# A sixteen-head attention with straight code in place of loops, and the out projection of each batch moved into the heads of the next

## The chip, the core and the metric

The kernel runs on one core of a Trainium2 chip. The metric is the device time of one execution in microseconds (us). Engines: TensorE (PE in the profile, PEld its weight loads), VectorE (DVE), ScalarE (ACT), GpSimd (POOL) and SyncE (SP), which issues the DMAs.

## The reference, cut to what matters

The network has four parts: a GRU over 256 time steps, a mixture of experts, an attention and a ternary gated feed-forward. Only the attention, in its wait structure, is changed. Per batch of 8, with 256 tokens, 16 heads of 32:

```python
xn = rms_norm(x, g_norm) * (1.0 + scale) + shift
q, k, v = split(xn @ W_qkv)             # 16 heads, each of width 32
q = rms_norm(q, g_q)
k = rms_norm(k, g_k)
attn = softmax(einsum('bhqd,bhkd->bhqk', q, k) * d ** -0.5)
o = einsum('bhqk,bhkd->bhqd', attn, v)  # -> (b, n, 512)
return o + o @ W_out
```

## The kernel before

The program is written by hand, engine by engine; each engine runs its own list in order, and semaphores couple the lists. The attention is one block of the program (lines 1459 to 1901). Values that need more than 16-bit precision are carried as a high and a low fp16 part, so most steps exist twice: ACT makes the high part (a copy that rounds), DVE or POOL the low part (a subtraction).

The attention goes batch by batch, and `batch(b)` overlaps two of them. For batch b it does the softmax side, head by head: `scores_t(b, h)` (transposed scores, L1547) two heads ahead, exp and its rounding on ACT (`softmax`, L1676 and L1681), the low part on DVE for heads 0 to 7 (`low_p`, L1783) and on POOL for heads 8 to 15 (L1876), then `values(b, h)` (L1562). After each four heads DVE divides by the sums (`normalise`, L1789 and L1791), PE transposes the four heads' outcome (`turn_out`, L1572), ACT and DVE split it (`high_out` L1686, `low_out` L1796). For batch b+1 it does the preparation between the heads, by tables of head numbers: six products of the q, k, v projection at heads 0, 1, 2, 3, 5 and 6 (`project`, L1494, taken out by ACT in `take_out`, L1645), the norms of q and k (with a square root on ACT, L1650, which needs another table than exp), their high and low parts (`high_qk` L1655, `low_qk` L1761 and L1762), the stacking of q and k by transposes at heads 8, 9, 10 and 13 (`stack`: L1512 on PE, q copied by DVE in L1767, k by ACT in L1659), and the row maxima of the scores from head 9 on (`scores` L1528 on PE, `maximum` L1772 on DVE). When all 16 maxima of batch b+1 are there, `turn_max` transposes them (L1534), ACT rounds them (L1664) and a DMA lays them into a row of q (L1467), which `scores_t(b+1, 0)` waits for.

At the end of a batch stands the out projection, in two halves of 24 products (`project_out`, L1586), with `scores_t(b+1, 0)` and `scores_t(b+1, 1)` between them. ACT takes each half out (L1712), DVE makes its low part (L1833). They use banks 5 and 6 of the PSUM, which `project` and `stack` also use:

```python
                    turn_out(b, 3)
                    if not last:
                        turn_max(b + 1)
                    project_out(b, 0, last)
                    if not last:
                        scores_t(b + 1, 0)
                        scores_t(b + 1, 1)
                    project_out(b, 1, last)
```

PE, POOL and SP run 7 batches as a hardware loop and the last as straight code; ACT and DVE loop over 6 and have two as straight code. The tables are `PROJECT_AT`, `STACK_AT`, `MAX_AT` and others, from line 1415.

## Time and profile before

| | us |
|---|---|
| median of 3 runs (lowest, highest) | 1812.58 (1811.27, 1815.29) |
| the profiled execution, its own time | 1806.46 |
| its span | 1804.7 |
| PE busy over the span | 1605.0 (89%) |
| DVE busy | 1182.3 (66%) |
| ACT busy | 918.2 (51%) |
| POOL busy | 599.8 (33%) |
| attention: first product of the projection to the first of the feed-forward | 1110.9 to 1573.4 |
| feed-forward | 1573.4 to 1804.7 |

Times within the span are counted from its start. PEclk is the granted clock of TensorE as a share of full speed: 1.00 is 2.4 GHz, 0.50 is 1.2 GHz. A row of the timeline gives start, duration, engine, line, operation, tile, and in brackets how long the engine had been idle and what ended that.

### The profile page before, as it was taken

Reading aid. Unit: us, or ns where it says so; the run is one execution under the profiler, and the core shown is the slowest. Engines: PE = TensorE matmul, PEld = TensorE weight load, DVE = VectorE, ACT = ScalarE, POOL = GpSimd, SP = SyncE. Lnnn points to the kernel's source line nnn. Section 1 sums busy time; section 2 is a strip of 40 time slices with the busy share of each in tenths; the row PEclk is TensorE's granted clock in tenths of the full one; section 3 lists DMA queues with packets and bytes.
Section 4 is the critical chain, followed back from the end, with each engine's and each line's share of the span. In section 5 each row is a group of like instructions: output and inputs, shape, how many; then the busy total and the mean of one; then the engine's idle time right before and its main releaser. Section 6 shows DMA issues by size and latency. Waiting matters only on the chain. (4 is left out here: it accounts for less than half of the span.)

```text
span 1804.7 us, 77596 instructions
## 1 busy us (share of the span) xinstructions
PE 1605.0 (89%) x32043; PEld 1221.5 (68%) x32043; DVE 1182.3 (66%) x4253; ACT 918.2 (51%) x3325; POOL 599.8 (33%) x1805
## 2 busy tenths in 40 slices
PE   6999999999999999996499956688888888699999
PEld 5999999999999999995366633355555555444444
DVE  5778787887877788886644445566655666573231
ACT  5555555555555566555155444466766666532130
POOL 0333333333333333334355434123322323580000
PEclk9999999999999999555699976788888989699999
DMA  4110101011100111003346352000000000130001
GB/s 171 49 29 8 53 17 45 24 33 42 46 22 5 43 49 46 25 23 117 110 159 237 131 183 98 1 1 0 0 0 0 0 0 1 33 109 18 30 0 47
DMA packets 45708, 90.37 MB, mean 50 GB/s; under 512 B 6736, under 2 KB 25296, under 8 KB 45392
## 3 DMA queue, kind: packets, MB, share of 16 engines
q1 hardware_dynamic: 38992, 64.89, 11.4%
q0 software_dynamic: 6400, 20.98, 3.4%
q8 instruction: 234, 3.83, 0.9%
q14 instruction: 82, 0.67, 0.1%
HBM read 66.90 MB, written 18.87 MB: 48 GB/s over the span
## 5 line engine op out<-in xcount | busy, mean ns | idle before, releaser
L402 PE MATMUL bank<-arena 128*128 128x8 f16 x12288 | 499.6, 170 | 7.6 <-issue 3.3
L405 PE MATMUL bank<-arena 128*128 128x16 f16 x12288 | 495.5, 182 | 2.2 <-issue 1.6
L402 PEld LDWEIGHTS bank<-arena 128*128 128x128 f16 x12288 | 410.1, 97 | 37.0 <-ACT bank L498 22.1
L405 PEld LDWEIGHTS bank<-arena 128*128 128x128 f16 x12288 | 411.6, 97 | 3.7 <-issue 2.6
L664 POOL TENSOR_TENSOR arena<-arena 128x16 f32<-128x16 f32 x512 | 116.7, 228 | 537.9 <-DVE arena L607 523.2
L468 ACT ACTIVATE arena<-arena 128x16 f32<-128x16 f32 x512 | 114.4, 223 | 304.2 <-DVE arena L586 304.0
L597 DVE TENSOR_TENSOR_SCAN arena<-arena,bank 128x64 f32<-128x64 f32 x512 | 147.1, 287 | 19.5 <-ACT arena L468 2.6
L1938 PE MATMUL bank<-arena 128*128 128x512 f16 x704 | 152.3, 379 | 1.7 <-PEq L1459 1.7
L586 DVE TENSOR_REDUCE arena<-bank 128x16 f32<-128x48 f32 x512 | 99.9, 195 | 80.8 <-PE bank L405 76.0
L375 PE MATMUL bank<-arena 128*128 128x256 f16 x1008 | 147.9, 273 | 1.5 <-issue 1.3
L1494 PE MATMUL bank<-arena 128*128 128x512 f16 x576 | 143.8, 405 | 4.5 <-DVE arena L1738 4.5
L603 DVE TENSOR_TENSOR_SCAN arena<-arena 128x48 f16<-128x48 f32 x512 | 134.2, 262 | 6.2 <-ACT arena L478 0.2
L478 ACT ACTIVATE arena<-arena 128x16 f32<-128x16 f32 x512 | 119.2, 233 | 22.9 <-DVE arena L597 4.4
L474 ACT ACTIVATE arena<-arena 128x16 f32<-128x16 f32 x512 | 110.3, 215 | 35.2 <-DVE arena L591 0.9
L1938 PEld LDWEIGHTS bank<-arena 128*128 128x128 f16 x704 | 68.8, 98 | 84.7 <-issue 1.9
L1876 POOL TENSOR_TENSOR arena<-arena 128x512 f16<-128x512 f32 x64 | 79.8, 1256 | 131.1 <-ACT arena L1681 131.0
L591 DVE TENSOR_REDUCE arena<-bank 128x16 f32<-128x48 f32 x512 | 106.2, 207 | 26.1 <-PE bank L405 1.1
L665 POOL COPY arena<-arena 128x16 f32<-128x16 f32 x512 | 118.4, 231 | 0.0
L607 DVE TENSOR_TENSOR_SCAN arena<-arena 128x48 f32<-128x48 f32 x512 | 117.3, 229 | 0.4
L1494 PEld LDWEIGHTS bank<-arena 128*128 128x128 f16 x576 | 59.4, 103 | 73.5 <-issue 16.6
L612 DVE TENSOR_TENSOR arena<-arena 128x16 f16<-128x16 f32 x512 | 95.8, 187 | 17.7
L666 POOL COPY arena<-arena 128x16 f32<-128x16 f32 x512 | 102.7, 201 | 0.0
(203 smaller groups left out, 2708.6 us busy)
## 6 DMA issues: line engine op xcount, KB each, us to landing
arena<-yrows SPq DMA_DIRECT2D x16, 512.0 KB, 4.1
arena<-in_wgu SPq DMA_DIRECT2D x48, 128.0 KB
arena<-in_xT SPq DMA_DIRECT2D x32, 128.0 KB, 2.3
hrows<-arena SPq DMA_DIRECT2D x16, 256.0 KB, 4.0
arena<-in_xtok SPq DMA_DIRECT2D x16, 256.0 KB
out_y<-arena SPq DMA_DIRECT2D x16, 256.0 KB, 2.0
arena<-in_wih SPq DMA_DIRECT2D x4, 768.0 KB, 5.5
arena<-in_whh SPq DMA_DIRECT2D x4, 768.0 KB, 6.0
```

What stands on the lines that cost most here:

```text
L375: mm = nc.tensor.matmul(bank[7][:, half_of(mt)], wihs[:, wp, k, mt, :], xs[:, xp, k, half_of(c)], start=(i % 24 == 0), stop=(i % 12 == 11) ...
L402: mm = nc.tensor.matmul(dst[:, j * B:(j + 1) * B, 1], w, h[:, 0], start=home not in opened, stop=False, skip_group_check=True)
L405: mm = nc.tensor.matmul(dst[:, j * B:(j + 1) * B, 1:3], w, h.rearrange("p a c -> p c a"), start=home not in opened, stop=False, skip_group ...
L468: A.activation(fn[:, HALF[g], 3], rzp[:, 0, HALF[g]], ACT.Sigmoid, scale=1 / SWX).then_inc(r_act[g], 1)
L478: A.activation(inh[:, HALF[g], 0], sn[:, HALF[g], 3], ACT.Tanh, scale=1 / SWX).then_inc(n_act[g], 1)
L597: V.tensor_tensor_scan(flat(sn[:, HALF[g]]), flat(fn[:, HALF[g]]), flat(gate_sums(t, 2, g)), 0.0, ALU.mult, ALU.add).then_inc(n_pre[g], 1)
L603: V.tensor_tensor_scan(flat(mv[:, t % 2, 0, HALF[g]]), flat(fh[:, HALF[g]]), flat(inh[:, HALF[g]]), 0.0, ALU.mult, ALU.add).then_inc(h_hi[ ...
L607: V.tensor_tensor_scan(flat(sh[:, HALF[g]]), flat(fh[:, HALF[g]]), flat(inh[:, HALF[g]]), 0.0, ALU.mult, ALU.add).then_inc(h_f32[g], 1)
L664: G.tensor_tensor(inh[:, HALF[g], 1], zeros[:, :], sh[:, HALF[g], 2], ALU.subtract)
L665: G.tensor_copy(inh[:, HALF[g], 2], sh[:, HALF[g], 2])
L1494: mm = nc.tensor.matmul(bank[5 + i % 2][:, :], xn[:, x_, k, half * P:(half + 1) * P], wqs[:, w_, k, col:col + D], start=(n == 0), stop=(n ...
L1938: mm = nc.tensor.matmul(bank[2 * a + u % 2][:, :], w12[:, mt, a, k, :], o2p[:, 2 * c:2 * c + 2, part, k, :], start=(n == 0), stop=(n == 2 ...
```

## The change

It does five things. (1) The loops of the attention become straight code on all five engines, so waits compare with constants. (2) `project_out(b-1, 0)` now stands at head 4 of batch b, and `project_out(b-1, 1)` at head 7, in banks 4 and 7; the last batch's own two halves stay at its end. (3) ACT and DVE take these halves out at heads 7 and 8 (`high_o2`, `low_o2`). (4) At heads 5, 9 and 13 `turn_out`, `high_out` and `low_out` come after the other work of that head instead of before it. (5) `oTp` has two buffers. The diff without blank lines:

```diff
@@ -1407,3 +1407,3 @@
 m = Mem(arena, mc.at)
-oTp = m.take([2, KT, S], F16)
+oTp = m.take([2, 2, KT, S], F16)
@@ -1419,2 +1419,4 @@
 LOW_AT = {6: (0, 1), 7: (2, 3)}
+OUT_AT = {4: 0, 7: 1}
+O2_AT = {7: (0,), 8: (1,)}
 STACK_AT = {8: (0,), 9: (1,), 10: (2,), 13: (3,)}
@@ -1473,3 +1475,3 @@
         load_max(0)
-        with sp.Fori(0, B - 1) as b:
+        for b in range(B - 1):
             load_max(b + 1)
@@ -1484,3 +1486,3 @@
-                pe.wait_ge(o2_lo, 2 * b + i - 1)
+                pe.wait_ge((qs_done, ks_done)[i], 4 * b)
             elif i >= 2:
@@ -1523,5 +1525,8 @@
                 pe.wait_ge(max_done, H * b + h - 1)
-            elif h == 1 and not first:
+            elif not first:
+                if h == 1:
-                pe.wait_ge(mT_done, b)
+                    pe.wait_ge(mT_done, b)
+                if b > 1:
+                    pe.wait_ge(o2_lo, 2 * (b - 2) + h + 1)
             for qt in range(2):
@@ -1575,3 +1580,3 @@
-        def project_out(b, jp, last):
+        def project_out(b, jp):
             if jp == 0:
@@ -1579,3 +1584,3 @@
-            pe.wait_ge((qs_done, ks_done)[jp], 4 * b + (4 if last else 8))
+                pe.wait_ge(max_done, H * min(b + 2, B))
             for a in range(2):
@@ -1585,4 +1590,4 @@
                     for k in range(KT):
-                        mm = nc.tensor.matmul(bank[5 + jp][:, a * S:(a + 1) * S],
-                                              wos[:, w_, k, j * P:(j + 1) * P], oTp[:, x_, k, :],
+                        mm = nc.tensor.matmul(bank[4 + 3 * jp][:, a * S:(a + 1) * S],
+                                              wos[:, w_, k, j * P:(j + 1) * P], oTp[:, b % 2, x_, k, :],
                                               start=(n == 0), stop=(n == 3 * KT - 1))
@@ -1598,4 +1603,2 @@
                     scores_t(b, h + 2)
-                if h % 4 == 1 and h > 4:
-                    turn_out(b, h // 4 - 1)
                 if not last:
@@ -1607,2 +1610,6 @@
                         scores(b + 1, i)
+                if h in OUT_AT and b > 0:
+                    project_out(b - 1, OUT_AT[h])
+                if h % 4 == 1 and h > 4:
+                    turn_out(b, h // 4 - 1)
                 values(b, h)
@@ -1613,7 +1620,7 @@
                 turn_max(b + 1)
-            project_out(b, 0, last)
-            if not last:
                 scores_t(b + 1, 0)
                 scores_t(b + 1, 1)
-            project_out(b, 1, last)
+            else:
+                project_out(b, 0)
+                project_out(b, 1)
@@ -1630,3 +1637,3 @@
         scores_t(0, 1, True)
-        with pe.Fori(0, B - 1) as b:
+        for b in range(B - 1):
             batch(b, False)
@@ -1685,3 +1692,7 @@
             act.wait_ge(oT_mm, 4 * b + q4 + 1)
-            A.activation(oTp[:, 0, q4, :], bank[q4 % 2][:, 0:S], ACT.Copy).then_inc(oTh_done, 1)
+            A.activation(oTp[:, b % 2, 0, q4, :], bank[q4 % 2][:, 0:S], ACT.Copy).then_inc(oTh_done, 1)
+        def high_o2(b, jp):
+            act.wait_ge(wo_mm, 2 * b + jp + 1)
+            A.activation(o2p_of(b, 0, jp), bank[4 + 3 * jp], ACT.Copy, scale=1 / SW).then_inc(o2_hi, 1)
@@ -1692,4 +1703,2 @@
                     softmax(b, h + 1)
-                if h % 4 == 1 and h > 4:
-                    high_out(b, h // 4 - 1)
                 if not last:
@@ -1703,2 +1712,7 @@
                         stack(b + 1, g)
+                if b > 0:
+                    for jp in O2_AT.get(h, ()):
+                        high_o2(b - 1, jp)
+                if h % 4 == 1 and h > 4:
+                    high_out(b, h // 4 - 1)
             high_out(b, 3)
@@ -1709,5 +1723,5 @@
                 norm_x(b + 2)
-            for jp in range(2):
-                act.wait_ge(wo_mm, 2 * b + jp + 1)
-                A.activation(o2p_of(b, 0, jp), bank[5 + jp], ACT.Copy, scale=1 / SW).then_inc(o2_hi, 1)
+            if last:
+                for jp in range(2):
+                    high_o2(b, jp)
@@ -1726,3 +1740,3 @@
         norm_x(1)
-        with act.Fori(0, B - 2) as b:
+        for b in range(B - 2):
             batch(b, False, True)
@@ -1795,5 +1809,10 @@
             dve.wait_ge(oTh_done, 4 * b + q4 + 1)
-            V.tensor_tensor(oTp[:, 1, q4, :], bank[q4 % 2][:, 0:S], oTp[:, 0, q4, :],
+            V.tensor_tensor(oTp[:, b % 2, 1, q4, :], bank[q4 % 2][:, 0:S], oTp[:, b % 2, 0, q4, :],
                             ALU.subtract).then_inc(oTl_done, 1)
+        def low_o2(b, jp):
+            dve.wait_ge(o2_hi, 2 * b + jp + 1)
+            V.scalar_tensor_tensor(o2p_of(b, 1, jp), bank[4 + 3 * jp], 1 / SW, o2p_of(b, 0, jp), ALU.mult,
+                                   ALU.subtract).then_inc(o2_lo, 1)
         def batch(b, last, more):
@@ -1807,4 +1826,2 @@
                     normalise(b, h // 4 - 1)
-                if h % 4 == 1 and h > 4:
-                    low_out(b, h // 4 - 1)
                 if not last:
@@ -1818,2 +1835,6 @@
                         low_qk(b + 1, n)
+                if b > 0:
+                    for jp in O2_AT.get(h, ()):
+                        low_o2(b - 1, jp)
+                if not last:
                     for g in STACK_AT.get(h, ()):
@@ -1822,2 +1843,4 @@
                         maximum(b + 1, i)
+                if h % 4 == 1 and h > 4:
+                    low_out(b, h // 4 - 1)
             normalise(b, 3)
@@ -1830,8 +1853,5 @@
                 norm_x(b + 2)
-            for jp in range(2):
-                dve.wait_ge(o2_hi, 2 * b + jp + 1)
-                V.scalar_tensor_tensor(o2p_of(b, 1, jp), bank[5 + jp], 1 / SW, o2p_of(b, 0, jp), ALU.mult,
-                                       ALU.subtract).then_inc(o2_lo, 1)
-        V.memset(rk[:, :, :], 0.0).then_inc(o2_lo, 2)
+            if last:
+                for jp in range(2):
+                    low_o2(b, jp)
@@ -1852,3 +1872,3 @@
         norm_x(1)
-        with dve.Fori(0, B - 2) as b:
+        for b in range(B - 2):
             batch(b, False, True)
@@ -1898,3 +1918,3 @@
             squares(0, i)
-        with pool.Fori(0, B - 1) as b:
+        for b in range(B - 1):
             batch(b, False)
```

On PE, heads 4 and 5 of a looped batch (L1494 projection, L1547 transposed scores, L1562 values, L1572 transposes of the outcome; REGISTER_ALU computes what a wait compares with). Before:

```order
L1543 REGISTER_ALU
L1547 MATMUL bank<-arena 128x256 x2
L1556 REGISTER_ALU
L1442 REGISTER_ALU
L1562 MATMUL bank<-arena 128x33 x12
L1543 REGISTER_ALU
L1547 MATMUL bank<-arena 128x256 x2
L1572 MATMUL bank<-cst,arena 128x128 x2
L1488 REGISTER_ALU
L1494 MATMUL bank<-arena 128x512 x12
L1442 REGISTER_ALU
L1562 MATMUL bank<-arena 128x33 x12
```

Now, batch 1, from the values of head 3 on (L1496 projection, L1552 transposed scores, L1567 values, L1577 transposes of the outcome, L1591 out projection):

```order
L1567 MATMUL bank<-arena 128x33 x12
L1552 MATMUL bank<-arena 128x256 x2
L1591 MATMUL bank<-arena 128x256 x24
L1567 MATMUL bank<-arena 128x33 x12
L1552 MATMUL bank<-arena 128x256 x2
L1496 MATMUL bank<-arena 128x512 x12
L1577 MATMUL bank<-cst,arena 128x128 x2
L1567 MATMUL bank<-arena 128x33 x12
L1552 MATMUL bank<-arena 128x256 x2
```

The first half of the out projection stands between `scores_t` and `values` of head 4, and the two transposes of the outcome have gone behind the projection of head 5.

On PE, heads 7 to 9 of batch 1 now (L1514 stacking, L1533 scores for the maxima):

```order
L1552 MATMUL bank<-arena 128x256 x2
L1591 MATMUL bank<-arena 128x256 x24
L1567 MATMUL bank<-arena 128x33 x12
L1552 MATMUL bank<-arena 128x256 x2
L1514 MATMUL bank<-id,arena 96x128 x16
L1567 MATMUL bank<-arena 128x33 x12
L1552 MATMUL bank<-arena 128x256 x2
L1514 MATMUL bank<-id,arena 96x128 x16
L1533 MATMUL bank<-arena 128x256 x4
L1577 MATMUL bank<-cst,arena 128x128 x2
```

The second half of the out projection stands at head 7, ahead of the first stacking; between the two stackings nothing was added on PE.

On DVE, heads 7 and 8 before (L1761 and L1762 low parts of q and k, L1789 and L1791 normalise, L1767 copy of the stacked q, L1796 low part of the outcome):

```order
L1761 COPY arena<-arena 128x16x32
L1762 TENSOR_TENSOR arena<-arena 128x16x32
L1789 RECIPROCAL arena<-bank 128x8
L1790 REGISTER_ALU
L1791 TENSOR_TENSOR arena<-bank,arena 128x2x128
L1767 COPY arena<-bank 96x1024
L1796 TENSOR_TENSOR arena<-bank,arena 128x256
L1767 COPY arena<-bank 96x1024
```

Now (L1775 and L1776, L1803 and L1805, L1781, and L1815 the low part of the out projection):

```order
L1776 TENSOR_TENSOR arena<-arena 128x16x32
L1815 SCALAR_TENSOR_TENSOR arena<-bank,arena 128x512
L1803 RECIPROCAL arena<-bank 128x8
L1805 TENSOR_TENSOR arena<-bank,arena 128x2x128
L1815 SCALAR_TENSOR_TENSOR arena<-bank,arena 128x512
L1781 COPY arena<-bank 96x1024 x2
L1786 TENSOR_REDUCE arena<-bank 128x2 x2
```

The copy of the stacked q stands behind the second L1815, which needs the second high part of ACT. On ACT, heads 8 and 9 now (L1683 and L1688 exp and its rounding, L1697 high part of the out projection, L1666 copy of the stacked k):

```order
L1683 ACTIVATE arena<-bank 128x512
L1688 ACTIVATE arena<-arena 128x512
L1697 ACTIVATE arena<-bank 128x512
L1683 ACTIVATE arena<-bank 128x512
L1688 ACTIVATE arena<-arena 128x512
L1666 ACTIVATE arena<-bank 96x1024
L1697 ACTIVATE arena<-bank 128x512
L1683 ACTIVATE arena<-bank 128x512
L1688 ACTIVATE arena<-arena 128x512
L1666 ACTIVATE arena<-bank 96x1024
```

That second high part stands behind the copy of the first stacked k.

## Rows read from the trace of the kernel before

**Rows 1.** windows, one per batch; columns as the first line says
```profile
core 0: us, PE busy (x) PEld busy (x) DVE busy (x) ACT busy (x) POOL busy (x), PEclk, DMA share, GB/s
...
1151.53:1200.88 49.35, 38.99 (x401) 23.00 (x402) 32.00 (x59) 35.18 (x57) 17.58 (x14) 0.88 0.01 2
1200.88:1255.22 54.34, 44.95 (x451) 28.19 (x450) 33.80 (x62) 36.56 (x60) 17.58 (x14) 0.91 0.00 0
1255.22:1310.76 55.54, 47.52 (x450) 30.64 (x449) 33.96 (x62) 36.57 (x60) 17.56 (x14) 0.84 0.00 0
...
1527.07:1573.37 46.30, 30.44 (x330) 21.00 (x331) 21.70 (x33) 23.48 (x45) 20.90 (x14) 0.63 0.00 1
```

**Rows 2.** timeline, all engines, start of batch 0: start, us, engine, line
```profile
1151.53 0.37 PE L1534 MATMUL bank<-cst,arena 128*32 128x128 f32 x1 [0.88 <-DVE arena L1772]
...
1154.68 1.03 PE L1547 MATMUL bank<-arena 97*128 97x256 f16 x4 [2.77 <-DMA arena<-arena]
1155.50 0.60 ACT L1676 ACTIVATE arena<-bank 128x512 f32<-128x512 f32 x1
...
1155.59 4.24 PE L1494 MATMUL bank<-arena 128*128 128x512 f16 x12
```

**Rows 3.** timeline, boundary of two looped batches
```profile
1201.98 4.93 PE L1586 MATMUL bank<-arena 128*128 128x256 f16 x24 [0.71 <-DVE arena L1796]
...
1207.19 2.79 PE L1586 MATMUL bank<-arena 128*128 128x256 f16 x24
...
1209.81 2.75 PE L1494 MATMUL bank<-arena 128*128 128x512 f16 x12
...
1210.73 1.28 ACT L1676 ACT_TABLE_LOAD   x1
```

**Rows 4.** timeline, TensorE alone, heads 4 and 5 of batch 0
```profile
1169.74 0.46 PE L1562 MATMUL bank<-arena 128*128 128x33 f16 x12
1170.56 0.39 PE L1547 MATMUL bank<-arena 97*128 97x256 f16 x2 [0.36 <-ACT arena L1676]
1172.53 0.69 PE L1572 MATMUL bank<-cst,arena 128*128 128x128 f32 x2 [1.57 <-DVE arena L1791]
1173.01 4.08 PE L1494 MATMUL bank<-arena 128*128 128x512 f16 x12
```

**Rows 5.** timeline, all engines, heads 6 to 15 of batch 0
```profile
1174.76 0.60 ACT L1676 ACTIVATE arena<-bank 128x512 f32<-128x512 f32 x1
...
1183.16 0.69 DVE L1762 TENSOR_TENSOR arena<-arena 128x512 f16<-128x512 f32 x1
...
1183.97 1.09 PE L1512 MATMUL bank<-id,arena 128*96 128x128 f16 x16 [1.17 <-DVE arena L1762]
...
1185.10 1.02 ACT L1659 ACTIVATE arena<-bank 96x1024 f16<-96x1024 f16 x1 [0.94 <-PE bank L1512]
...
1185.74 1.08 PE L1512 MATMUL bank<-id,arena 128*96 128x128 f16 x16
...
1189.71 0.68 DVE L1767 COPY arena<-bank 96x1024 f16<-96x1024 f16 x1
...
1190.30 3.07 DVE L1772 TENSOR_REDUCE arena<-bank 128x2 f32<-128x512 f32 x5
```

**Rows 6.** window, end of batch 0, columns as in rows 1
```profile
1189.71:1200.88 11.17, 8.80 (x127) 5.82 (x125) 11.05 (x22) 6.99 (x11) 5.73 (x5) 0.94 0.01 3
```

**Rows 7.** timeline, TensorE alone, heads 8 to 10 of batch 2
```profile
1292.78 1.94 PE L1512 MATMUL bank<-id,arena 128*96 128x128 f16 x16 [1.18 <-DVE arena L1762]
...
1298.85 1.06 PE L1512 MATMUL bank<-id,arena 128*96 128x128 f16 x16
```

**Rows 8.** timeline, all engines, last batch
```profile
1535.62 0.59 ACT L1676 ACTIVATE arena<-bank 128x512 f32<-128x512 f32 x1
...
1564.45 7.23 PE L1586 MATMUL bank<-arena 128*128 128x256 f16 x48 [0.93 <-DVE arena L1796]
```

**Rows 9.** the page: matmuls of the unrolled recurrence, with idle time before them
```profile
L405 PE MATMUL bank<-arena 128*128 128x16 f16 x12288 | 495.5, 182 | 2.2 <-issue 1.6
```

## The prediction

> **What bounds the kernel now.** I read the windows by batch first, with the transpose of the maxima (L1534) as the mark between batches. From the first mark at 1151.53 to the eighth at 1527.07 the attention takes 375.54 us; batch 0, which has no out projection before it, takes 49.35, the six from 1200.88 on take 326.19, or 54.37 on average (54.34 and 55.54 are two of them) [rows 1]. No engine is full in them: PE is busy 44.95 us of 54.34, ACT 36.56, DVE 33.80. So what counts is which wait ends last in each stretch, and for that I read the timelines. I write r for us after a batch's mark.
>
> At the boundary of two looped batches the first half of the out projection takes 4.93 us, because PE comes out of a thin stretch at the half clock, the second 2.79; the next projection starts at r = 8.93 [rows 3]. In batch 0 nothing stands there: PE waits 2.77 us for the DMA that carries the maxima, starts the scores at r = 3.15 and the projection at r = 4.06, where it takes 4.24 instead of 2.75 at the half clock [rows 2, 3].
>
> At heads 4 and 5 PE waits 0.36 for an exp and 1.57 for the division, and the clock falls: the projection after it takes 4.08 [rows 4]. Before the first stacking it waits 1.17 for the last low part of q and k [rows 5]. From the copy of the third stacked q (r = 38.18 in batch 0) to the mark DVE is busy 11.05 of 11.17 us [rows 5, 6]: whatever comes late at that copy is late at the mark, one for one.
>
> **The change, step by step.**
>
> 1. Boundary. Every batch from 1 to 6 now begins as batch 0 does: transpose, DMA wait, two heads of scores, projection. If the two halves cost nothing elsewhere, each would take 49.35, and the six would give 326.19 - 6 x 49.35 = 30.1 us.
>
> 2. First half at head 4. It adds 24 products at the full clock, 2.62 us (the second half at the boundary starts at 1207.19 and the next work at 1209.81 [rows 3]). It stands where PE waited 0.36 and 1.57, and with the transposes behind the projection there is no wait left, so the projection should take 2.75 instead of 4.08 [rows 3, 4]: 0.36 + 1.57 + 1.33 = 3.26 us of cover. By hand from batch 0: values of head 4 at r = 20.84 (18.21 before), projection of head 5 from 21.37 to 24.12 (25.56 before). What bounds next is the ACT chain over the square root, whose two table loads do not move: exp of head 6 at r = 23.23 as before [rows 5].
>
> 3. Second half at head 7. PE reaches it at r = 27.8 and leaves at 30.4; the last low part of q and k comes at about 31.96 (32.32 before, the end of L1762 [rows 5]), since the projection of head 5 came 1.4 earlier but DVE's order allows only 0.4. So the half is covered, and the first stacking starts at 32.08 instead of 32.44.
>
> 4. Taking out at heads 7 and 8. This is the step that is not covered. DVE may copy the first stacked q only after its second low part, which waits for ACT's second high part, which stands behind ACT's copy of the stacked k. From the end of stacking at r = 33.17: copy of k 0.92 to the next start (1.02 long [rows 5]), high part 0.60, low part 0.69, copy of q 0.68, with gaps r = 36.1. The last two durations are those of a DVE operation of 128x512 (0.69) and of the q copy [rows 5]. Before, the second stacking started at 1185.74, r = 34.21 [rows 5]. So it is 1.9 us late, and PE, which has done the scores of head 11 by 33.8, stands 2.3 us, after another 1.1 before the first stacking.
>
> 5. What 1.9 us become at the third copy. If the clock stays at full speed, part is caught up in a stretch where DVE had waited: the third copy starts at 39.0, 0.85 late. If it falls, the second stacking takes 1.94 instead of 1.08 [rows 5, 7], the first two scores and the transposes behind it double too, and I get 40.7 to 41.2, which is 2.5 to 3.0 late. A wait of 1.57 brought the fall at head 5 [rows 4], and 1.24 and 1.18 of wait with two products between brought it in batch 2, but not in batch 0 [rows 5, 7]. The new pause is longer than both, so I take the fall, 2.6 us. Bounds: 0.85 without it, and 3.6 (1.92 with two stackings of 0.86 longer each) if nothing is caught up.
>
> 6. Batch 0 gets only the new place of the transposes: -0.4 us, from the earlier low parts (step 3); between 0 and -1.
>
> 7. Last batch. Exp of head 0 started 8.55 us after the mark (1535.62 - 1527.07) and will at about 3.9, as in batch 0 (1155.50 - 1151.53 = 3.97) [rows 1, 2, 8]. The two halves of batch 6 come back at heads 4 and 7, where ACT sets the pace; at the half clock the first takes up to 4.4 us. By hand the exp of head 10 comes 1.5 earlier, the transposes of head 9 2.7. The block of 7.23 us at the end stays [rows 8]. I take -2.8; bounds -4.6 (all covered) and 0.
>
> 8. Straight code. The waits lose their register instructions; a wait that was ended by DVE shows no delay from them, so nothing. ACT loses a table load of 1.28 us at the start of the looped batches [rows 3]. It stood behind ACT's second half of the out projection; in its new place the start of a batch waits for the DMA, so nothing comes on top of step 1. The Trainium skill ("ScalarE: Activation LUTs", What ACT_TABLE_LOAD costs) puts a load at about 2.7 us; the trace has 1.28 and decides, and by neither figure does the sum change, as the load is gone from the path.
>
> The jump back to the head of PE's loop shows no pause: the last half of the out projection starts at 1207.19, takes 2.79, and the next batch's projection starts at 1209.81 [rows 3]. So the jumps give nothing. The Trainium skill ("Runtime: NRT & Kernel Launch", Instruction fetch mechanics) says the opposite of this row, that a taken branch out of the loaded window stops the engine for a fetch; by that rule straight code would give a pause per batch on top, and no run here shows one.
>
> Sum for the profiled execution: -30.1 + 6 x 2.6 - 0.4 - 2.8 = -17.7, so 1806.46 - 17.7 = 1788.8. The median of the runs is 6.1 above that execution; with the same shift it is 1812.58 - 17.7 = **1794.9 us**.
>
> **The rivals.**
>
> A. The clock does not fall at the new pause. For it: in batch 0 two waits of 1.2 left it alone [rows 5]. Against: the pause is one piece of 2.3. Then 6 x 0.85 in place of 6 x 2.6: -28.2, 1784.4 us.
>
> B. Slower: the clock falls at head 9 and does not come back before the mark. From there to the mark PE has 3 stackings, 16 scores, 7 values, 5 transposed scores and 3 transposes; at the half clock a stacking is left after about 1.74 (an estimate from the 1.94 of [rows 7]), and everything but the scores comes to 11.0. With DVE's 16 maxima, 0.6 each (five in 3.07 [rows 5]), no longer beside that but between, the mark comes at r = 36.1 + 11.0 + 9.6 = 56.7. That is 6 x 2.33 more than now, less 3.2 from steps 6 and 7: about +11, 1823 us. It decides from a period of 54.9 on (54.37 + 3.2/6). Against it: in batch 2 the clock fell at the first stacking and the third took 1.06 again [rows 7], since PE is then busy without a pause.
>
> C. No gain, or slower too: straight code stops for its fetches. PE has some 900 instructions a batch, products and loads together (451 and 450 [rows 1]). One pause a batch as long as the DMA wait of 2.77 [rows 2] would be 19.4 over seven batches, which ends at no change, 1814 us; a second one makes it 1834. Against it: the recurrence is 256 unrolled steps, and its 12288 products of one kind waited 1.6 us in all for issue [rows 9].
>
> D. The changed order loses more of the cover (steps 2, 5 and 7 at their bad ends): -30.1 + 6 x 3.6 + 0 = -8.5, 1804.1 us.
>
> **How the numbers follow.** A difference of 0.2% (3.6 us) is about what can be told from none. Chances: forecast 0.57, A 0.24, D 0.09, B 0.06, C 0.02, and 0.02 for no visible change. Faster: 0.57 + 0.24 + 0.07 of D = 0.88; same 0.04 (half of C, a part of D, and no visible change); slower 0.08 (B and the rest). The range takes in A with a little of step 7 (-30) and D: 1782.5 to 1804.
>
> **What would show it.** Right: the gap from mark to mark about 52 us in batches 1 to 6; PE waiting some 2.3 us for L1781 before the second stacking, and stackings of 1.9 us there; projection of head 5 at 2.75; no table load at the start of batches. If the second stacking starts by r = 34.5, step 4 is wrong; if the stacking after the pause takes 1.1, it is A; waits for issue on PE inside a batch would be C. A projection of head 5 that still takes over 4 us would break step 2.

## The result, and the profile after

The changed kernel takes **1790.84 us** (median of 4 runs, 1787.47 to 1794.16) against 1812.23 (4 runs); the ratio is 0.9877, with a 95% interval of 0.9854 to 0.9900. It is 21.4 us faster; 17.7 was forecast (1794.9), and the range of 1782.5 to 1804 holds it.

The two profiled executions differ by less, 1789.96 against 1806.46 us. Their attention, from the first product of the projection to the first of the feed-forward, took 462.45 us before (1110.92 to 1573.37) and takes 440.93 now (1115.90 to 1556.83): 21.5 less. But it began 4.98 later, in code that the change doesn't touch. The same kernel profiled once more began its attention at 1120.52; of the kernel before there is one trace only, so how far its start scatters isn't known. So below I compare the attention alone wherever a trace is read, and whole times only by their ratio to the kernel before on the same chip.

The windows by batch after, which answer to [rows 1] (mark to mark, the last row the feed-forward; columns as in the first line):

```profile
core 0: us, PE busy (x) PEld busy (x) DVE busy (x) ACT busy (x) POOL busy (x), PEclk, DMA share, GB/s
...
1156.16:1205.95 49.79, 39.50 (x402) 25.04 (x402) 32.42 (x59) 35.12 (x58) 18.00 (x14) 0.86 0.01 1
1205.95:1259.13 53.18, 45.33 (x449) 29.85 (x450) 34.05 (x62) 35.15 (x59) 18.01 (x14) 0.87 0.01 2
1259.13:1310.05 50.92, 43.07 (x450) 28.36 (x449) 33.96 (x62) 35.15 (x60) 18.02 (x14) 0.90 0.01 1
1310.05:1359.80 49.75, 41.67 (x449) 27.09 (x450) 33.79 (x62) 34.98 (x60) 18.01 (x14) 0.93 0.01 2
1359.80:1412.80 53.00, 45.15 (x449) 29.79 (x450) 34.05 (x62) 35.15 (x59) 18.02 (x14) 0.86 0.01 2
1412.80:1463.75 50.95, 43.16 (x451) 28.36 (x450) 33.97 (x62) 35.08 (x59) 18.02 (x14) 0.90 0.00 1
1463.75:1513.44 49.69, 41.63 (x449) 27.07 (x449) 33.79 (x62) 35.05 (x60) 18.00 (x14) 0.94 0.01 2
1513.44:1556.83 43.39, 28.66 (x329) 20.81 (x330) 21.56 (x33) 23.40 (x45) 20.09 (x14) 0.69 0.01 1
```

Batches 1 to 6 (six rows from 1205.95 on) take 307.49 us together, 51.25 on average, where they took 326.19. Their busy times hardly differ from each other, yet they come in three kinds, about 53, 51 and 49.7, in the same order twice; PEclk differs with them.

The start of batch 2, in the timeline of all engines, which answers to [rows 2, 3]:

```profile
1259.13 0.39 PE L1539 MATMUL bank<-cst,arena 128*32 128x128 f32 x1
...
1262.20 1.03 PE L1552 MATMUL bank<-arena 97*128 97x256 f16 x4 [2.67 <-DMA arena<-arena]
1262.84 0.60 ACT L1683 ACTIVATE arena<-bank 128x512 f32<-128x512 f32 x1 [1.03 <-PE bank L1552]
...
1263.13 3.84 PE L1496 MATMUL bank<-arena 128*128 128x512 f16 x12
```

It begins as batch 0 did: the DMA of the maxima is waited for (2.67), the projection stands at r = 4.00 and runs partly at the half clock, and no table load stands ahead of the first exp. Heads 4 to 8 of the same batch, which answer to [rows 4, 5]:

```profile
1276.88 2.78 PE L1591 MATMUL bank<-arena 128*128 128x256 f16 x24
...
1279.50 0.46 PE L1567 MATMUL bank<-arena 128*128 128x33 f16 x12
...
1280.02 2.75 PE L1496 MATMUL bank<-arena 128*128 128x512 f16 x12
...
1282.61 0.38 PE L1577 MATMUL bank<-cst,arena 128*128 128x128 f32 x2
```

The first half of the out projection (L1591) is followed without a wait; the projection of head 5 takes 2.75, and the transposes (L1577) wait for nothing. Then the place of step 4:

```profile
1290.56 1.09 PE L1514 MATMUL bank<-id,arena 128*96 128x128 f16 x16 [0.78 <-DVE arena L1776]
...
1291.69 1.02 ACT L1666 ACTIVATE arena<-bank 96x1024 f16<-96x1024 f16 x1 [0.82 <-PE bank L1514]
...
1292.61 0.58 ACT L1697 ACTIVATE arena<-bank 128x512 f16<-128x512 f32 x1
...
1293.22 0.69 DVE L1815 SCALAR_TENSOR_TENSOR arena<-bank,arena 128x512 f16<-128x512 f32 x1 [1.55 <-ACT arena L1697]
...
1293.83 0.68 DVE L1781 COPY arena<-bank 96x1024 f16<-96x1024 f16 x1
...
1294.56 1.09 PE L1514 MATMUL bank<-id,arena 128*96 128x128 f16 x16 [2.22 <-DVE arena L1781]
```

Read downwards: stacking ends at 1291.65; ACT copies k (L1666), only then makes the second high part (L1697); DVE its low part (L1815), then the copy of q (L1781); and PE, after 2.22 us of waiting, stacks again at r = 35.43. In batch 1 the same pause ends with the clock down (the timeline of TensorE alone):

```profile
1242.31 1.94 PE L1514 MATMUL bank<-id,arena 128*96 128x128 f16 x16 [2.22 <-DVE arena L1781]
...
1246.09 1.91 PE L1514 MATMUL bank<-id,arena 128*96 128x128 f16 x16
```

The granted clock of the two second stackings, batch 1 and batch 2, in the windows: 0.50 is 1.2 GHz, 1.00 is 2.4 GHz.

```profile
1242.31:1244.25 1.94, 1.94 (x17) 1.89 (x18) 0.69 (x1) 0.00 (x0) 1.01 (x1) 0.50 0.00 0
1294.56:1295.65 1.09, 1.09 (x18) 1.07 (x19) 0.40 (x1) 0.00 (x0) 1.01 (x1) 1.00 0.00 0
```

### The profile page after: what moved, and what is told of

Read it like the earlier page. It is cut to its first block and busy times, and to the rows that moved or that the text cites. A ratio compares the mean times of both kernels' runs of the same rounds, so it can differ in the third digit from the quotient of the medians.

```text
span 1788.2 us, 76589 instructions
## 1 busy us (share of the span) xinstructions
PE 1593.9 (89%) x32043; PEld 1222.2 (68%) x32043; DVE 1184.0 (66%) x4252; ACT 911.5 (51%) x3320; POOL 601.9 (34%) x1805
## 5 line engine op out<-in xcount | busy, mean ns | idle before, releaser
L1496 PE MATMUL bank<-arena 128*128 128x512 f16 x576 | 142.7, 402 | 4.5 <-DVE arena L1752 4.5
L665 POOL COPY arena<-arena 128x16 f32<-128x16 f32 x512 | 118.4, 231 | 0.0
L1496 PEld LDWEIGHTS bank<-arena 128*128 128x128 f16 x576 | 58.3, 102 | 74.8 <-issue 14.9
L612 DVE TENSOR_TENSOR arena<-arena 128x16 f16<-128x16 f32 x512 | 95.9, 187 | 17.7
L1797 DVE TENSOR_TENSOR arena<-arena 128x512 f16<-128x512 f32 x64 | 45.3, 708 | 90.8 <-ACT arena L1688 90.7
```

What stands on the lines that cost most here:

```text
L665: G.tensor_copy(inh[:, HALF[g], 2], sh[:, HALF[g], 2])
L1496: mm = nc.tensor.matmul(bank[5 + i % 2][:, :], xn[:, x_, k, half * P:(half + 1) * P], wqs[:, w_, k, col:col + D], start=(n == 0), stop=(n ...
```

## Experiments

Each run was made from the changed kernel unless it says from before. "Attention" is the length defined above, of one profiled execution. The runs were made on several chips: on that of e5 to e8 the kernel before takes 1801.47 us, on the others 1812 to 1814, and there is no trace of it on that one. The ratios check the comparison: the time that each implies against before and the difference in attention agree within 2.5 us (e5 7.4 and 9.1, e6 25.0 and 25.3, e7 43.2 and 40.8, e8 50.1 and 51.9), for e10 within 5.4. A summary first, in us:

```
kernel                                  ratio to before (95%)      attention   mean of batches 1-6
before                                                              462.45      54.37
changed                                 0.9877 (0.9854 to 0.9900)   440.93      51.25
changed, once more (e9)                 0.9894 (0.9878 to 0.9911)   441.75      51.27
e1 straight code alone                  0.9956 (0.9935 to 0.9976)   456.62      52.91
e2 straight code and transposes         0.9911 (0.9881 to 0.9941)   446.14      51.44
e3 taking out reordered                 0.9800 (0.9761 to 0.9839)   427.04      48.58
e4 filler in the pause                  0.9886 (0.9851 to 0.9922)   440.65      51.00
e5 thin out projection                  0.9959 (0.9943 to 0.9974)   453.38      53.43
e6 transposes back                      0.9861 (0.9836 to 0.9886)   437.13      50.54
e7 e3 and filler in the DMA wait        0.9760 (0.9737 to 0.9782)   421.68      47.44
e8 e3 and projection in the DMA wait    0.9722 (0.9697 to 0.9746)   410.51      45.92
e10 e8, transposes back                 0.9766 (0.9733 to 0.9799)   414.63      46.92
```

**e1, straight code alone.** From before: the five loops unrolled, nothing else.

```diff
-                with act.Fori(0, B - 2) as b:
+                for b in range(B - 2):
                     batch(b, False, True)
```

> The kernel before, with its five hardware loops written as straight code and nothing else; what is computed is unchanged. Read from the trace of before: a looped batch has one exp table load of 1.28 us behind ACT's second half of the out projection, and batch 6, whose ACT part was straight already and had no such load, took 52.47 us where its neighbours took 53.9 to 55.6. Theory 1 (the load stood on the path at the boundary, the rest of the looping cost nothing): five loads fewer, each worth 1.3 to 1.9, so 1803 to 1806 us against 1812.2. Theory 2 (step 8 of the prediction read strictly, straight code in itself is worth nothing): 1812. Theory 3 (fetches): slower than 1816.

Measured: ratio 0.9956, attention 5.8 us shorter. The start of batch 1, all engines:

```profile
1215.95 2.75 PE L1494 MATMUL bank<-arena 128*128 128x512 f16 x12
1216.15 0.60 ACT L1712 ACTIVATE arena<-bank 128x512 f16<-128x512 f32 x1 [2.46 <-PE bank L1586]
1216.64 0.59 ACT L1676 ACTIVATE arena<-bank 128x512 f32<-128x512 f32 x1
```

The exp now starts 0.49 after the high part, where the load of 1.28 stood [rows 3]. By windows, batches 1 to 5 take 52.5 to 53.4 against 53.9 to 55.6, between 1.2 and 2.5 less each, 8.7 in the six together; batch 0, the last one and the projection ahead of the first mark give 2.9 back. So theory 1 holds in place and size, and the reading that straight code is worth nothing falls. In batches 1 to 5 the gain is 1.8 each, 0.5 more than the load; what the 0.5 is, these runs don't tell. No fetch shows: in the kernel before, ACT's last high part ends at 1210.71 and the load starts at 1210.73. The Trainium skill ("Runtime: NRT & Kernel Launch", Instruction fetch mechanics) would have a jump back out of the loaded window cost one; no run here shows whether the heads of these loops lay outside it, so these rows are neither for that rule nor against it. The predicted sum was not touched by this, since it took batch 0 as its base, which has the gain in it.

**e2, transposes behind the other work, in addition.** From e1; PE as shown, ACT and DVE alike:

```diff
-                        if h % 4 == 1 and h > 4:
-                            turn_out(b, h // 4 - 1)
...
+                        if h % 4 == 1 and h > 4:
+                            turn_out(b, h // 4 - 1)
                         values(b, h)
```

> As the run with straight code alone, and in addition the transposes of the outcome, with their high and low parts, behind the other work of heads 5, 9 and 13; the out projection stays at the boundary. Theory 1 (the chain over the square root bounds heads 5 to 8, only about 0.4 us a batch come through): 2 to 4 us less than straight code alone. Theory 2 (the wait of 1.57 and the slow projection of 4.08 go entirely): 2.9 a batch, 20 us less than straight code alone. By theory 1 the projection of head 5 takes 2.75 all the same.

Measured: 10.5 us less attention than e1, between the theories, and neither is right in size. Of that 8.8 us are in batches 1 to 6 and 1.6 in the last batch. In batches 1 to 6 the first stacking comes at r = 34.1 to 34.9, where e1 has 34.9 to 35.5, about 0.9 earlier; the rest of the batch takes 17.1 instead of 17.2 to 17.9. Only the first part is what theory 1 counts. The windows of batch 3 in both, e1 first:

```profile
1312.58:1365.29 52.71, 44.23 (x451) 29.33 (x450) 34.14 (x62) 35.12 (x60) 18.00 (x14) 0.91 0.01 1
```

```profile
1319.20:1370.56 51.36, 43.30 (x449) 29.07 (x449) 34.00 (x62) 34.93 (x60) 18.02 (x14) 0.93 0.01 2
```

DVE and ACT do the same work in 1.35 us less. How the second part divides between the order at head 9 and the clock, these two runs don't tell; e10 shows what that order can cost.

**e3, the taking out reordered.** ACT's second high part ahead of its copy of k, DVE's copy of q ahead of the second low part:

```diff
 # ACT
-                            for g in STACK_AT.get(h, ()):
-                                stack(b + 1, g)
                         if b > 0:
                             for jp in O2_AT.get(h, ()):
                                 high_o2(b - 1, jp)
+                        if not last:
+                            for g in STACK_AT.get(h, ()):
+                                stack(b + 1, g)
 # DVE
+                            for g in STACK_AT.get(h, ()):
+                                stack(b + 1, g)
                         if b > 0:
                             for jp in O2_AT.get(h, ()):
                                 low_o2(b - 1, jp)
                         if not last:
-                            for g in STACK_AT.get(h, ()):
-                                stack(b + 1, g)
```

> The changed kernel, with two things swapped at head 8: ACT makes the second high part of the out projection before it copies the stacked k, and DVE copies the first stacked q before it makes the second low part. Theory (step 4: the taking out delays the second stacking by 1.9 us): the wait of 2.22 before the second stacking falls below 0.7, no stacking there takes 1.94, and batches 1 to 6 take 49.2 to 49.9 each instead of 51.25 on average: 8 to 12 us less than the changed kernel, about 1781. Rival (the two low parts cost DVE 1.4 us in a full stretch anyway, and the wait only moves to the third stacking): less than 3 us.

Measured: 0.9800, attention 13.9 us shorter than the changed kernel's. The timeline of batch 1, all engines:

```profile
1240.85 1.09 PE L1514 MATMUL bank<-id,arena 128*96 128x128 f16 x16 [0.78 <-DVE arena L1777]
1241.08 0.58 ACT L1697 ACTIVATE arena<-bank 128x512 f16<-128x512 f32 x1
...
1241.89 0.68 DVE L1782 COPY arena<-bank 96x1024 f16<-96x1024 f16 x1
...
1242.62 1.09 PE L1514 MATMUL bank<-id,arena 128*96 128x128 f16 x16
```

The copy of q (L1782) starts 1.04 after the stacking it needs has begun, and the second stacking follows at 1242.62, 1.77 after the first instead of 4.00, with no wait. The batches take 48.04 to 49.36. The gain is above the forecast of 8 to 12 (16.0 us in batches 1 to 6, of which the last batch gives 1.7 back); step 4 is confirmed by removing it.

**e4, filler in the pause.** 36 products on constants ahead of the second stacking of batches 1 to 6:

```diff
+                            if h == 9 and b > 0:
+                                filler(36)
                             for g in STACK_AT.get(h, ()):
                                 stack(b + 1, g)
```

> The changed kernel, with 36 products of 128 columns on constants, into an unused part of a bank, before the second stacking of batches 1 to 6: some 2.0 us of work in the pause of 2.22, read by nobody. In the changed kernel the six batches take 53.2, 50.9, 49.75, 53.0, 50.95 and 49.7 with the same pause in each, and differ in where the granted clock falls. Theory (the differences are the clock's alone): all six at 49.6 to 50.0, stackings at 1.09, 8 to 10 us less than the changed kernel, about 1782. Rival (the differences come from elsewhere, or the filler delays the stacking): no gain, or slower by up to 2 us a batch where the clock is at half already.

Measured: attention 0.3 us shorter, ratio as that of the changed kernel. In the timelines of TensorE, batch 1 at head 9 and the start of batch 2:

```profile
1247.38 1.09 PE L1514 MATMUL bank<-id,arena 128*96 128x128 f16 x16 [0.21 <-DVE arena L1788]
```

```profile
1264.61 1.03 PE L1552 MATMUL bank<-arena 97*128 97x256 f16 x4 [2.67 <-DMA arena<-arena]
1265.55 5.16 PE L1496 MATMUL bank<-arena 128*128 128x512 f16 x12
```

The filler does what it should: every second stacking takes 1.09, and from there to the mark all six batches need 14.2 us (in the changed kernel 16.8, 15.5 or 14.2). Half of the theory stands: in this stretch the three kinds of batches are the clock's. The expected gain doesn't come, because the first projection of batches 2 to 6 now runs at the half clock nearly from end to end (5.16 in batch 2, where the changed kernel has 3.84; its range there is 3.8 to 4.9) and the first stacking is at 32.8 to 33.0 instead of 31.4 to 32.2. In both kernels the clock is down when this projection starts; with the filler it comes back later. What the clock gave at one wait it took at the next.

**e5, a thin out projection.** Of 24 products a half, 4 are made in batches 0 to 6, so their out projection is left out for the most part:

```diff
+                                if b < B - 1 and 0 < n < 3 * KT - 1:
+                                    n += 1
+                                    continue
```

> The changed kernel; of the 24 products of each half of the out projection of batches 0 to 6 only 4 are made (the first and last of each of its two groups of 12), so the out projection of these batches is not computed in full; taking out, waits and the last batch are unchanged. It takes 2.2 us of PE work from head 4 and again from head 7 of batches 1 to 6. Theory (steps 2 and 3: both halves lie in waits that the chain over the square root and the low parts of q and k set anyway): the first stacking still at r = 31.4 to 32.4, attention within 3 us of the changed kernel's 440.9, though the clock may fall at the new gaps (up to +1 a batch). Rival (PE's own work sets these heads): stackings some 2 to 4 us earlier and 12 to 25 us less.

Measured: attention **12.5 us longer** with less work. Batch 2 in the windows, against 50.92 us in the changed kernel, and two rows of its TensorE:

```profile
1250.37:1304.68 54.31, 42.93 (x411) 26.88 (x410) 34.04 (x62) 35.12 (x59) 18.02 (x14) 0.81 0.01 1
```

```profile
1275.25 0.39 PE L1552 MATMUL bank<-arena 97*128 97x256 f16 x2 [1.35 <-ACT arena L1686]
...
1283.26 1.80 PE L1514 MATMUL bank<-id,arena 128*96 128x128 f16 x16 [1.53 <-DVE arena L1779]
```

The first stacking is at r = 31.4 to 32.9, where it was with all 24 products (31.4 to 32.4). Where the first projection takes as long, so does all up to it: batch 1 has 4.88 and r = 32.46 (changed kernel 4.87 and 32.35), batch 3 has 3.77 and 31.36 (batch 2 of the changed kernel 3.84 and 31.43). So the halves cost PE nothing there, as steps 2 and 3 said. But TensorE now waits, in batch 2, 1.35 for an exp, 0.56, 0.81 and then 1.53 for the low parts, and the clock is down at both stackings of every batch (1.77 to 1.94; PEclk 0.81 against 0.90). The gaps that the out projection fills are also what lets the clock fall; that was worth more than I allowed (1 us a batch; it is 2.2).

**e6, the transposes back.** The three pieces moved in e2 put back ahead in the changed kernel.

> The changed kernel, with the transposes of the outcome and their high and low parts back ahead of the other work of heads 5, 9 and 13. Theory (with the out projection at head 4 the division is done before PE gets to the transposes, r = 20.9 against 21.2, so they wait for nothing): projection of head 5 at 2.75 in batches 1 to 6; within 3 us of the changed kernel, of which up to 1.5 for batch 0, where the wait of 1.57 comes back. Rival (their place was worth what it was worth without the move of the out projection, 10.5 us of attention in the run with it alone): 8 to 11 us slower than the changed kernel.

Measured: attention 3.8 us shorter than the changed kernel's, ratio the same within its interval. The projection of head 5 needs no cover from them any more (2.75 in batches 1 to 6). So in the changed kernel their place is worth nothing, although it was worth 10.5 without the out projection at heads 4 and 7. Two things are behind that, and this run shows them together: nothing waits at head 5, and at head 9 the transposes and their high part fall into the pause before the second stacking (2.00 here), their low part beside that stacking. The 3.8 us go with the clock: around the second stacking it falls in one batch of six, where in the changed kernel it does in four. The gains of the parts don't add: straight code 5.8, transposes 10.5, out projection 19.5 if it comes alone (456.62 - 437.13) and 5.2 if it comes last (446.14 - 440.93).

**e7 and e8, the wait for the DMA.** Both start from e3. In e7, 22 products on constants stand in the wait of 2.67 at the mark; in e8 it is 8 of the 12 products of a projection, with the other 4 behind the scores (the diff is e8's, on PE):

```diff
                         turn_max(b + 1)
+                        if b + 2 < B:
+                            pe.wait_ge(xn_hi, b + 3)
+                            pe.wait_ge(qs_done, 4 * (b + 2))
+                            project_part(b + 2, 0, ((0, 0), (1, 0)), 0)
                         scores_t(b + 1, 0)
                         scores_t(b + 1, 1)
+                        if b + 2 < B:
+                            pe.wait_ge(xn_lo, b + 3)
+                            project_part(b + 2, 0, ((0, 1),), 2 * KT)
```

In e8 ACT rounds the input before `high_out(b, 3)`, and DVE makes its low part before that of v.

> The kernel with the taking out reordered at head 8, and in addition 22 products of 128 columns on constants in the wait for the DMA of the maxima (2.67 us, PE at the half clock then), read by nobody. Theory (the clock comes back a while after PE has become busy, so work in the wait brings it back earlier): the first projection of a batch takes 2.75 to 3.4 instead of 3.8 to 4.3, some 1 us less in each of batches 1 to 6, about 6 us less than 1779. Rival (it comes back at its own time, or the filler at the half clock runs past the DMA): no gain or slower.

> The kernel with the taking out reordered at head 8, and in addition the first projection of the batch after next, split: its 8 products on the high part of the normalised input stand in the wait for the DMA of the maxima, its 4 on the low part behind the first two heads' scores; ACT rounds that input at the end of the head loop, DVE makes the low part ahead of that of v. Nothing computed is left out. Theory (the wait of 2.67 is the last uncovered piece of the boundary, and the start of a batch is bound by PE): the scores of head 2 at r = 5.5 to 6 instead of 8.1, the first stacking 1.5 to 2.5 earlier, 8 to 14 us less than 1779. Rival (the chain of exp over the heads sets the first stacking, or DVE's stretch before the mark takes it back): less than 4 us.

Measured, e7: attention 5.4 us shorter than e3's. The start of batch 2, TensorE:

```profile
1246.93 2.40 PE L1599 MATMUL bank<-id 128*128 128x128 f16 x22
1249.80 0.61 PE L1552 MATMUL bank<-arena 97*128 97x256 f16 x4 [0.47 <-DMA arena<-arena]
1250.74 2.76 PE L1496 MATMUL bank<-arena 128*128 128x512 f16 x12 [0.33 <-DVE arena L1759]
```

The filler began at the half clock (22 products in 2.40), did not reach the DMA's end, and the projection takes 2.76 where e3 has 4.3 to 5.1: where the clock is down by the start of the wait, work in it brings it back earlier. So it goes in batches 1 to 3 (projection 3.21, 2.76, 2.76; batches of 46.5 to 47.0). In batches 4 to 6 the clock is still up at the mark, the filler runs faster and leaves more of the wait, and the clock falls all the same. The start of batch 5:

```profile
1388.13 1.39 PE L1599 MATMUL bank<-id 128*128 128x128 f16 x22
1390.96 0.61 PE L1552 MATMUL bank<-arena 97*128 97x256 f16 x4 [1.44 <-DMA arena<-arena]
1391.89 4.45 PE L1496 MATMUL bank<-arena 128*128 128x512 f16 x12 [0.32 <-DVE arena L1759]
```

These three take 48.2 us each, little less than in e3 (48.9, 48.3 and 48.0). So theory and rival each hold in half of the batches.

Measured, e8: ratio 0.9722, attention 16.5 us shorter than e3's, more than the forecast of 8 to 14, and 30.4 shorter than the changed kernel's. The start of batch 3, all engines:

```profile
1290.54 2.58 PE L1498 MATMUL bank<-arena 128*128 128x512 f16 x8
...
1293.76 0.61 PE L1555 MATMUL bank<-arena 97*128 97x256 f16 x4 [0.64 <-DMA arena<-arena]
...
1294.20 1.03 PE L1498 MATMUL bank<-arena 128*128 128x512 f16 x4
...
1295.07 0.38 PE L1555 MATMUL bank<-arena 97*128 97x256 f16 x2
```

The scores of head 2 stand at r = 4.72 (4.5 to 5.7 in batches 1 to 6) instead of 8.0 to 9.0 in e3, the first stacking comes 2.4 earlier than there on average, and the batches take 45.5 to 46.5. This version beats both kernels.

**e9, the changed kernel once more.**

> The changed kernel once more, in nothing different, for how far its batches and its stretch ahead of the attention scatter. Theory (the six batches differ only by where the clock falls, which shifts from execution to execution): the wait of 2.22 in each of batches 1 to 6, periods again of about 49.7, 50.9 and 53.1 in another order, attention at 436 to 446 us; the ratio to before again 0.985 to 0.99. Rival (the periods belong to the batches): the same periods in the same order, attention at 440.9 within 0.5.

Measured: batches 1 to 3 are these, in the windows:

```profile
1211.30:1264.58 53.28, 45.41 (x451) 29.83 (x450) 34.07 (x62) 35.22 (x59) 18.04 (x14) 0.85 0.01 2
1264.58:1315.53 50.95, 43.13 (x451) 28.41 (x450) 33.97 (x62) 35.13 (x60) 18.03 (x14) 0.90 0.01 1
1315.53:1365.26 49.73, 41.65 (x450) 27.07 (x450) 33.80 (x62) 35.05 (x60) 18.03 (x14) 0.94 0.01 2
```

and batches 4 to 6 take 52.98, 50.95 and 49.70. The theory falls and the rival holds for the batches: their kinds come in the same order, though the attention began 4.6 us later. Its other half, attention within 0.5 us, misses a little: 0.8 longer, 0.5 ahead of the first mark and 0.3 in batch 0.

**e10, e8 with the transposes back.**

> The kernel with the taking out reordered and the first projection in the wait for the DMA, and in addition the transposes of the outcome back ahead of the other work of heads 5, 9 and 13. Theory (once the out projection fills head 4 their place is worth nothing): attention within 3 us of 410.5. Rival (in a shorter batch the copies by ACT and DVE at head 9 stand in the way again): 5 us slower or more.

Measured: attention 4.1 us longer than e8's, a little outside the 3 us, and what the rival describes is in the trace. Head 9 of batch 3, all engines:

```profile
1337.95 0.37 ACT L1703 ACTIVATE arena<-bank 128x256 f16<-128x256 f32 x1
...
1338.35 0.43 DVE L1821 TENSOR_TENSOR arena<-bank,arena 128x256 f16<-128x256 f32 x1 [1.29 <-ACT arena L1703]
...
1338.69 0.68 DVE L1792 COPY arena<-bank 96x1024 f16<-96x1024 f16 x1
...
1339.42 1.09 PE L1517 MATMUL bank<-id,arena 128*96 128x128 f16 x16 [0.81 <-DVE arena L1792]
```

DVE waits 1.29 for the high part of the outcome, makes its low part (L1821) and only then copies the second stacked q (L1792), for which the third stacking waits 0.81. It does so in all six batches, and stands 2.83 behind the second stacking instead of 2.11: 4.3 us. Another 1.3 is the clock, down at the fourth stacking of batch 2; batch 0 and the stretches around it give some back. So the place of the transposes is worth something again once the pause is gone, about 0.7 us a batch; in e6 the pause before the second stacking hid that.

## Why the prediction was right, and where it was off

The direction, the size and the mechanism held; step by step:

- **Step 1, boundary: right.** Batches 1 to 6 begin as batch 0 did, with the wait for the DMA (2.67 against 2.77) and the projection at r = 3.9 to 4.0. It takes 3.8 to 4.9 us, by how soon the clock is back, where batch 0 had 4.24.
- **Step 2, first half at head 4: right.** No wait behind it, projection of head 5 at 2.75. e5 shows that its 24 products are free there.
- **Step 3, second half: right.** The first stacking was forecast at r = 32.08 after a wait of 1.1; it comes at 31.4 to 32.4, 31.75 on average, after 0.78.
- **Step 4, the taking out: right, and the heart of it.** The second stacking was forecast 4.02 after the first (36.1 - 32.08), behind a pause of 2.3; measured 4.00 and 2.22, in all six batches. e3 shows it by taking it away.
- **Step 5, what it becomes at the mark: mis-sized.** I took 2.6 us for every batch, with the clock down at once. It was down at the second stacking in two batches, fell during the work right behind it in two, and not at all in two: 53.2 and 53.0, 50.9 and 50.95, 49.75 and 49.7. So batches 1 to 6 came 11.4 us above six times 49.35 instead of 15.6, 4.2 less. Half of that isn't this step's: the second stacking stands at r = 35.75 on average where 36.1 was forecast, which is 2.1 us over six batches and comes from the earlier first stacking (steps 1 to 3). From there to the mark 15.85 was forecast and 15.50 measured, the other 2.1. The price of the clock's fall was too low (51.95 a batch forecast with it, 53.1 measured; 50.2 without it, 49.7 measured), and the full fall came in two batches of six. These two misses nearly cancel, so that the average lies within 0.7 us of the forecast is in part luck: no batch took 52. What failed is the reading "The new pause is longer than both, so I take the fall": the length of one wait doesn't say whether the clock falls. Rival A, with no fall, is a third of the batches.
- **Step 6, batch 0: wrong sign.** +0.44 instead of -0.4. Its first stacking came 0.7 earlier, more than the 0.4 reasoned, but with the clock down (1.94). It isn't scatter alone: batch 0 takes 49.2 to 49.8 in the four traces with the transposes in the old place (before, e1, e6, e10) and 49.8 to 50.3 in the eight with the new one.
- **Step 7, last batch: right.** -2.91 (46.30 to 43.39) against -2.8. The transposes of head 9 come 3.2 earlier instead of 2.7; the closing block takes 7.59 instead of 7.23.
- **Step 8, straight code: right in the sum.** No wait of PE for issue appeared in the batches, and the 5.8 us that straight code alone gives (e1), five table loads for the most part, were inside step 1. The figure of about 2.7 us that step 8 sets against the trace's 1.28 counts more than the load: the Trainium skill ("ScalarE: Activation LUTs", What ACT_TABLE_LOAD costs) has 1.28 for the load itself, as in this trace, and 1.38 for a drain. No drain shows here: from the end of ACT's work at 1210.71 to the exp at 1212.02 it is 1.31. Nor does the row at PE's jump say "the opposite" of the fetch rule, as long as it isn't known whether the loop's head lay in the loaded window. Rivals B and C showed nothing: after every fall behind the pause the clock was back by the fourth stacking (1.06), 6 us or more ahead of the mark.

Against the 21.5 us of attention: 18.7 from batches 1 to 6, 2.9 from the last, 0.35 from ahead of the first mark, less 0.44 from batch 0.

## What to carry to other kernels

When work is moved into another stage, follow each of its consumers as well as the work: here the products were free and the two small copies behind them, in the wrong order on two engines, cost 14 us. Before changing several things, ask which of them cover the same wait, since their gains then overlap, and a wait that is left can hide what an order costs until it is removed (e6 and e10). And a wait of TensorE has two prices, its length and the clock after it: in the same wait filler gave 5.4 us and work that is needed anyway 16.5.

## What the runs showed of the hardware that I had not expected

TensorE with less to do was slower: 20 products fewer at two places in each of batches 1 to 7 made the attention 12.5 us longer, with the granted clock at 0.81 to 0.83 per batch instead of 0.86 to 0.94. Filling one wait kept the clock up behind it and brought it back later behind the next, for a gain of 0.3 us (5.16 instead of 3.84 for a projection). Filling the wait for the DMA brought the clock back in the three batches in which it was down by the start of that wait (projection 2.76 to 3.21); in the three in which it was up it fell behind the filler all the same (4.45 to 4.5). And the pattern of falls was not random: with an equal pause in each batch it repeated every three batches, in both executions of the changed kernel and, with other lengths, in e5 (53.7, 54.3, 52.1, then 53.9, 54.4, 52.2). What sets it, no run here shows.
